# The output rows of a fast-weight loop: ScalarE copies them out of PSUM and GpSimd scales them with a power, in place of VectorE's reciprocal and scaling

## The reference, cut to what matters

```python
# for each chunk of 64 rows, per head (8 heads in two pairs of batches):
gate = ki @ w0_;  hb = ki @ w2_;  ...            # gradients of three 128x128 matrices
w1g, w0g, w2g = newtonschulz5(...), ...          # two steps of X = a X + (b A + c A A) X, bf16
w_ = (w_ + wg) / norm(w_) * wn                   # the three state matrices
oi = silu(qi @ w0_) * (qi @ w2_) @ w1_           # output rows of the chunk
# after the scan, per row of 128:
out = out * rsqrt(mean(out * out) + 1e-5) * onorm_w
out = out @ W_proj;   x = x + ga * out
```

## Time and profile before

| what | value |
|---|---|
| time, median of 3 runs | 1015.84 us (1014.73 to 1016.3) |
| the profiled execution's own time | 1013.95 us |
| its span (first to last instruction) | 1011.9 us |
| TensorE clock granted over the span | 0.997 of full speed |
| the recurrence, steps 0 to 7 and finish | up to about 400 us of the span |

### The profile page before, as it was taken

The page is one execution under the profiler, slowest core; times in us unless marked ns, Lnnn a source line. Parts: engine busy times, 40 slices in busy tenths (PEclk is TensorE's granted clock), DMA queues, the critical chain, the costliest instruction groups (busy, mean ns, idle before and its releaser), DMA issues.

```text
span 1011.9 us, 24653 instructions
## 1 busy us (share of the span) xinstructions
PE 954.8 (94%) x9502; PEld 718.5 (71%) x9502; DVE 695.5 (69%) x2072; ACT 576.7 (57%) x1537; POOL 435.5 (43%) x391
## 2 busy tenths in 40 slices
PE   5887999999999999999999999999999999999988
PEld 3565887887886755666556769786878687868646
DVE  4889989989989942213222577876787678777884
ACT  2667888888888852222214275655565556555541
POOL 1320240340532711101011666775677567779720
PEclk9999999999999999999999999999999999999999
DMA  9250000000000001900001422222222222212202
GB/s 312 74 197 3 2 0 0 0 0 0 0 2 2 2 1 30 344 11 1 1 0 42 91 58 54 68 60 53 53 65 64 53 54 63 64 38 48 95 3 85
DMA packets 32811, 52.94 MB, mean 52 GB/s; under 512 B 7760, under 2 KB 17744, under 8 KB 31824
## 3 DMA queue, kind: packets, MB, share of 16 engines
q1 hardware_dynamic: 32720, 51.69, 18.5%
HBM read 22.57 MB, written 2.10 MB: 24 GB/s over the span
## 4 chain that ended last, share of the span: by engine, by line
PE 46%; DVE 8%; ACT 2%; issue 2%; POOL 1%; DMA 0%; SPq 0%; DVEq 0%; POOLq 0%
PE quad L2151 9%; PE quad L1740 8%; PE quad L2110 8%; PE quad L2054 5%; PE quad L2170 5%; PE quad L2184 4%; DVE act_probs L2509 2%; DVE wq_wo L2524 2%; PE quad L2248 1%; DVE x_pairs L2541 1%; ACT act_probs L2407 1%; PE quad L2118 1%; PE quad L1626 1%; PE quad L2073 1%; ACT hT L1639 1%
## 5 line engine op out<-in xcount | busy, mean ns | idle before, releaser
L2763 POOL TENSOR_TENSOR act_probs<-act_probs,rden 128x512 f32<-128x512 f32 (+3 forms) x128 | 169.3, 1329 | 103.3 <-DVE rden L2529 103.3
L2407 ACT ACTIVATE act_probs<-act_probs,neg_max 128x256 f32<-128x256 f32 (+3 forms) x256 | 141.1, 553 | 84.5 <-DVE neg_max L2509 84.1
L2110 PEld LDWEIGHTS quad<-hT,ug_queries 128*128 128x128 f32 x1024 | 122.6, 192 | 14.4 <-issue 7.7
L2110 PE MATMUL quad<-hT,ug_queries 128*128 128x128 f32 x1024 | 124.7, 275 | 1.2 <-ACT act_probs L2417 0.5
L1740 PE MATMUL quad<-hT,ug_raw_switch 128*128 128x512 f32 x256 | 113.9, 595 | 0.0
L1755 DVE SCALAR_TENSOR_TENSOR act_probs<-quad,ws_up,silu_keys 128x512 f32<-128x512 f32 x32 | 24.0, 750 | 98.2 <-ACT silu_keys L1750 98.2
L1750 ACT ACTIVATE silu_keys<-quad,ws_gate 128x512 f32<-128x512 f32 x32 | 22.0, 688 | 118.6 <-PE quad L1740 118.6
L1740 PEld LDWEIGHTS quad<-hT,ug_raw_switch 128*128 128x128 f32 x256 | 47.5, 190 | 54.9 <-issue 54.8
L2151 PE MATMUL quad<-down_raw_out,ug_raw_switch 128*128 128x256 f32 (+3 forms) x256 | 79.6, 439 | 4.7 <-DVE neg_max L2509 4.7
L2151 PE MATMUL quad<-silu_keys,ug_raw_switch 128*128 128x256 f32 (+3 forms) x256 | 79.6, 439 | 3.7 <-DVE neg_max L2509 3.7
L2529 DVE RECIPROCAL rden<-den 128x2 f32<-128x2 f32 x128 | 20.2, 158 | 82.9 <-ACT act_probs L2407 82.7
(11 more groups left out here) (339 smaller groups left out, 2309.8 us busy)
## 6 DMA issues: line engine op xcount, KB each, us to landing
rope_swapped<-gate SPq DMA_DIRECT2D x120, 64.0 KB, 2.0
ug_raw_switch<-gate SPq DMA_DIRECT2D x60, 128.0 KB, 2.3
ug_raw_switch<-in_wmod SPq DMA_DIRECT2D x4, 512.0 KB, 7.1
x_pairs<-in_x SPq DMA_DIRECT2D x4, 512.0 KB, 7.5
x_rows<-x_pairs SPq DMA_DIRECT2D x8, 256.0 KB, 5.0
wq_wo<-in_wq_nopeT SPq DMA_DIRECT2D x1, 2048.0 KB, 8.6
wq_wo<-in_wo SPq DMA_DIRECT2D x1, 2048.0 KB, 13.1
ug_queries<-in_switch_w SPq DMA_DIRECT2D x1, 2048.0 KB, 8.1
```

The lines of the kernel that those rows point to most:

```text
L2110: mm = nc.tensor.matmul(out[:, P * i:P * i + P], w[:, kt, HP * half + i, :], in_order(k.hT[:, kt, b, cols], i), start=(kt == 0), stop=(kt ...
L2407: nc.scalar.activation(tile, tile, ACT.Exp, bias=neg_max[:, r, e:e + 1], scale=-1.0, accum_out=den[:, r, e:e + 1])\
L2763: nc.gpsimd.tensor_tensor(tile, tile, rden[:, t % RING, :].unsqueeze(2).to_broadcast([P, 2, cols]), ALU.mult)\
```

## The change

In each step from 1 to 7 the row scale of chunk t-1 is made and applied elsewhere:

- ScalarE, right behind the four squares, copies bank 6 into `o_n` (128x512) and writes mean plus epsilon to `o_rt` with an Identity activation. The square root further down its stream is gone.
- VectorE's reciprocal and scaling are gone from the steps.
- GpSimd raises `o_rt` to the power -0.5 (`invert_out`, 128x4) and multiplies `o_n` by it in place (new `norm_out`, 128x512). Both stand after `apply_rates` and ahead of `copy_h` and `add_out`; in step 7 after `move_q` and ahead of `add_out(5)`.

```diff
             def square_out(c, at=6):
...
                 op.then_inc(s["o_squared"], 1)
-
-            def root_out(c):
-                act.wait_ge(s["o_squared"], c + 1)
-                nc.scalar.activation(o_rt[:], o_ss[:], ACT.Sqrt, bias=o_eps[:, 0:1], scale=1.0 / HD).then_inc(s["o_rooted"], 1)
+                if at == 6:
+                    nc.scalar.activation(o_n[:].rearrange("p i h d -> p (i h d)"), bank[at][:], ACT.Copy)
+                    act.wait_ge(s["o_squared"], c + 1)
+                    nc.scalar.activation(o_rt[:], o_ss[:], ACT.Identity, bias=o_eps[:, 0:1], scale=1.0 / HD).then_inc(s["o_rooted"], 1)
...
-            def norm_out(c, at=6):
-                if at == 6:
-                    dve.wait_ge(s["o_rooted"], c + 1)
-                    nc.vector.reciprocal(o_r[:], o_rt[:]).then_inc(s["o_inverted"], 1)
+            def norm_out(c, at):
                 dve.wait_ge(s["o_inverted"], c + 1)
...
                     polynomial(AA1, q)
-                    if not first and n == NORM_OUT:
-                        norm_out(t - 1)
...
+            def norm_out(c):
+                pool.wait_ge(s["o_inverted"], c + 1)
+                to = o_n[:].rearrange("p i h d -> p (i h) d")
+                nc.gpsimd.tensor_tensor(to, to, bc(o_r[:], U, HD), ALU.mult).then_inc(s["o_normed"], 1)
+
             def invert_out(c):
                 pool.wait_ge(s["o_rooted"], c + 1)
                 nc.gpsimd.tensor_tensor(o_r[:], o_rt[:], k.neg_half[:, 0:U], ALU.pow).then_inc(s["o_inverted"], 1)
...
                     apply_rates(t + 1)
+                    if not first:
+                        invert_out(t - 1)
+                        norm_out(t - 1)
                 else:
                     pool.wait_ge(norms.xn_done, norms.groups[LN0B].end)
                     may_move(t, first)
                     move_q()
+                    invert_out(t - 1)
+                    norm_out(t - 1)
```

More of the change, by code:

```diff
@@ L1034, in step @@
                         square_out(t - 1)
[L1035 to L1039, removed]
+                    elif ph == TURN_OUT and n == 1 and not first:
+                        take_out(t - 1)
                     elif ph == START and first:
```

## The result

| | before | after |
|---|---|---|
| median of 4 runs | 1016.06 us (1014.73 to 1016.3) | 1022.75 us (1021.11 to 1024.01) |
| ratio | | 1.0068, 95% interval 1.0049 to 1.0087 |
| profiled execution: own time, span | 1013.95, 1011.9 us | 1021.11, 1019.3 us |
| TensorE clock granted over the span | 0.997 | 0.993 |

The change costs 6.9 us (5.0 to 8.8). The forecast was slower, 1025.5 us with a range from 1019.0 to 1028.5: right in sign and in range, 2.75 us too high.

A forecast was written before the change was run, and what follows sets the result against it. TensorE and VectorE run neck and neck, TensorE later by 0.24 us in steps 1 to 5. Terms 1.9 - 0.36 + 7.7 + 0.5 = 9.7 us on 1013.95 give 1023.7; with 1.9 for the median, 1025.5 us, range 1019 to 1028.5.

The forecast's parts named there:

- VectorE's pair worth nothing in steps 1 to 5, 0.36 us in step 6: Removed reciprocal and scaling: only idle time gained in steps 1 to 5, 0.36 us gained once in step 6.
- ScalarE's part nothing: Added copy and Identity: hidden in steps 1 to 5, perhaps 0.1 us each in steps 6 and 7, left out.
- GpSimd's pair ahead of the copy, 0.38 a step, 1.9 us: Steps 1 to 5: power and scaling delay the input-row copy, so TensorE's projection starts 0.38 us late; 1.9 lost, bounds 1.0-3.0.
- The end of step 7, 7.7 us: GpSimd's delayed queue runs beside VectorE's sums of squares, the engines taking turns; TensorE waits, 7.7 us lost, bounds 5 to 9.
- one sum of squares slips in behind each: End of step 7: one VectorE sum per GpSimd instruction, eight in all, GpSimd delayed by 7 x 0.21 us.
- the bound of 5: Lower bound of the loss at the end of step 7: 5 us if some sums pass two at a time.
- The clock, 0.5 us: After TensorE's stall at the end of step 7, a lower granted clock loses 0.5 us, bounds 0 and 1.6.
- VectorE keeping the ports: Rival, end of step 7: VectorE keeps the ports once it has them, time near 1019.5 us; chance 0.10.
- The end being hidden: Rival: step 7's end is hidden, only the loop counts, +1.5 us, 1017.4, no difference to be told; chance 0.05.
- VectorE setting every step: Rival: VectorE's 0.81 us comes off each of seven steps, 5.7 us faster, 1010.1 us; chance 0.04.
- GpSimd slowing VectorE in the loop: Rival: power and scaling block VectorE's scalings of Y, seven times 2.2 us on top, about 1041; chance 0.03.

The follow-up runs named there:

- no_scale: Kernel before without VectorE's reciprocal and scaling and ScalarE's square root in steps 1 to 7, ScalarE copying the bank instead; ratio 0.9988, in place -0.6 us.
- copy_first: Changed kernel with GpSimd's copy of the input rows ahead of the power and scaling in steps 1 to 5; ratio 1.0062, in place +7.5 us.
- loop_only: Changed kernel with the change kept in steps 1 to 6 only, step 7 as in the kernel before; ratio 0.9989, in place +1.2 us.
- tail_wait: Changed kernel with GpSimd waiting in step 7, before fly_down's ten adds, until VectorE has scaled the last states; ratio 0.9986, in place +0.2 us.
- wait_only: Kernel before with one wait added: in step 7 GpSimd, after move_q, waits for chunk 6's sums of squares; ratio 1.0050, in place +4.8 us.

## Why the prediction was right

**VectorE's pair worth nothing in steps 1 to 5, 0.36 us in step 6.** Right: 0.33 in place, and no_scale has it without GpSimd's work.

**ScalarE's part nothing.** Right for the loop (copy_first: 0.02 a step). Missed was step 7, where 0.15 was won: in the trace of before the root takes 0.18 us of ScalarE at 340.75, right ahead of a copy for which a weight load at 341.58 waits 0.17 us; in the changed kernel that wait is gone. loop_only, which keeps the root there, has the wait of 0.17 and wins 0.03.

**GpSimd's pair ahead of the copy, 0.38 a step, 1.9 us.** Right in place and kind, 0.31 a step and 1.55 in all; the projection's weight load waits 0.23 to 0.30 us where the waits are marked, against 0.3 to 0.5 foretold. The mis-sized piece was the gap between power and scaling: taken as 0.18 from the scaling of q and k, measured 0.08. The pair cost 2.07 instead of 2.22. With 2.07 the same sum gives 0.23 a step, so 0.08 of the measured 0.31 are left without a source.

**The end of step 7, 7.7 us.** Right mechanism, shown from three sides: without the company the loss is gone (tail_wait), with the company but without the change's work it is there (wait_only), with the change's loop alone it isn't (loop_only). The queue moved by 340.00 - 332.52 = 7.5 us in a trace whose project_out of step 7 stood 0.54 earlier, so by 8.0 against project_out, where 8.1 was predicted. The third group's scaling, though, came 6.3 us later (14.77 behind project_out, before 8.51) and not 7.7. The step that was off is "one sum of squares slips in behind each": from 351.71 on eight pieces of GpSimd's work let eleven sums begin, and these lengthened GpSimd's by 0.5 us in all, not by seven times 0.21. So GpSimd ended some 1.0 us and the sums some 1.5 us sooner than predicted, and TensorE's first transposes were 6.05 us late (13.84 behind project_out, before 7.79). That three sums passed as the second behind one piece of GpSimd's is the case of the bound of 5, not of the value taken.

**The clock, 0.5 us.** Too small: 3.47 us from the first transposes to the next product, where the kernel before took 2.56 (359.23 to 361.79) with a wait in it, and 0.17 more in that product: 1.1 us, and 1.9 in copy_first. The assumption that most of the slow stretch lies under waits for VectorE did not hold, because TensorE had a backlog of 16 transposes and no wait among them.

**Sum.** Predicted 9.7, in place 8.2: 0.35 less in the loop, 0.15 less in step 7, and at the end 6.05 + 1.08 = 7.13 for 7.7 + 0.5. The two misses at the end, 1.65 too much for the turns and 0.6 too little for the clock, partly cancel, which is luck. The remaining 1.2 us up to the 2.75 of the medians lie outside the places: 0.4 in the second layer and the rest in the scatter told above.

**The rivals.** VectorE keeping the ports: the sums alternate with GpSimd's instructions, so no. The end being hidden: TensorE idled 5.88 us. VectorE setting every step: no_scale. GpSimd slowing VectorE in the loop: the six scalings of Y in step 4 took 3.67 us beside GpSimd's power and scaling, as they did before without them, and the steps of copy_first, with all of the moved work in them, grew by 0.02. By the Trainium skill (Perfetto Trace Analysis, section "Optimizing Scalar/DVE Operations") moving work between these two engines may not help since they share a read port; the trace agrees only in the narrower form of the Trainium skill's SBUF — State Buffer, section "Who interferes with whom": instructions with an input from PSUM kept their times, those with both inputs in on-chip memory, 0.28 us long, took 1.34.

## What to carry to other kernels

Work that is moved to an idle engine's queue moves everything behind it there; ask for each of those instructions not only who waits for it but also beside whom it will now run. A short VectorE instruction with both inputs in on-chip memory paid here the length of whatever GpSimd had in hand, so a chain of small reductions on the critical path wants GpSimd idle, and a single wait on GpSimd bought that (8.0 us in place in the changed kernel, 0.9 in the kernel before). And a wait in front of a queue is best put between pieces that can run before it.

## What was not expected of the hardware

- The alternation is not strict. Three of the four short sums, at 352.64, 355.40 and 361.84, begin together with an instruction of GpSimd that stood 0.08 us behind its predecessor; where GpSimd's next followed without a gap (354.01, 358.10), the sum had to wait at once. A gap of 0.08 us in GpSimd's queue was worth a whole turn to VectorE. wait_only has the same at 352.70 and 359.14.
- The cost is one-sided: the sums grew from 0.28 to 1.34, GpSimd's adds of 1.27 to 1.31 to at most 1.45.
- After the same stall of 5.9 us the same instructions of TensorE took 0.8 us longer in one kernel than in another (copy_first against the change), because the clock had fallen later within the stall and came back later.
- At the same idle of 1.99 us ahead of 400 the clock fell in four of the twelve traces (0.58 in tail_wait) and stayed in the others (1.00 in before).
